# The order of score tiles and value products in the third window of each head

## What is computed

```python
q = (x @ w_q)...   # 32 heads of 128
k = (x @ w_k)...   # 8 key heads, each shared by 4 query heads
v = (x @ w_v)...
lk = ((x @ w_lq) @ w_lk)...   # 32 latent key heads
lv = (x @ w_lv)...            # 32 latent value heads
q, k, lk = rope(q), rope(k), rope(lk)
attn = causal_attn(q, k, v)      # softmax(q k^T * scale) v
lat = causal_attn(q, lk, lv)
return attn @ w_o + lat @ w_lo
```

## Time and profile before

| what | value |
|---|---|
| time, median of 3 runs | 2036.35 us (2035.51 to 2037.13) |
| profiled execution: time | 2036.75 us |
| profiled execution: span of the trace | 2035.0 us |
| PE / PEld busy | 99% / 86% of the span |
| DVE / ACT / POOL busy | 72% / 59% / 44% |
| mean granted TensorE clock | 0.998 |
| HBM traffic | 40 GB/s over the span |

### The profile page before, as it was taken

One profiled execution on the slowest core, in us unless ns is written; L12 is line 12 of the kernel. 1 busy time (PEld: TensorE's weight loads), 2 busy tenths in 40 slices (PEclk: granted clock), 3 DMA queues, 4 the chain that ended last, 5 costly groups with the idle time before them and its releaser, 6 DMA issues.

```text
span 2035.0 us, 33416 instructions
## 1 busy us (share of the span) xinstructions
PE 2018.2 (99%) x11716; PEld 1753.1 (86%) x11716; DVE 1457.1 (72%) x2884; ACT 1203.7 (59%) x2505; POOL 889.9 (44%) x684
## 2 busy tenths in 40 slices
PE   8999999999999999999999999999999999999989
PEld 7888888888888888888888888888888888888877
DVE  7677776776777767777677776777776776777777
ACT  4666556565565656666566565666566565565651
POOL 5444544444443454444534454444544444443422
PEclk9999999999999999999999999999999999999999
DMA  3111111111111111112111111111111111111031
GB/s 108 47 34 44 48 28 38 34 49 37 38 39 39 33 44 37 44 28 49 33 44 37 39 39 28 49 34 44 48 28 41 32 49 39 37 39 38 23 68 42
DMA packets 101797, 83.78 MB, mean 41 GB/s; under 512 B 28152, under 2 KB 73848, under 8 KB 101632
## 3 DMA queue, kind: packets, MB, share of 16 engines
q1 hardware_dynamic: 101632, 81.65, 15.7%
HBM read 79.26 MB, written 2.36 MB: 40 GB/s over the span
## 4 chain that ended last, share of the span: by engine, by line
PE 97%; DVE 2%; ACT 1%; POOL 0%; issue 0%; DMA 0%; DVEq 0%; ACTq 0%
PE bankT L587 13%; PE scores L514 12%; PE scores L516 12%; PE scores L515 12%; PE bankX L514 9%; PE bankX L516 9%; PE bankX L515 9%; PE bankO L516 7%; PE bankO L515 7%; PE bankO L514 7%; PE scores L707 0%; PE scores L553 0%; DVE rot_half L1124 0%; DVE xnT_lo L1097 0%; ACT probs L876 0%
## 5 line engine op out<-in xcount | busy, mean ns | idle before, releaser
L815 ACT ACTIVATE PT_hi<-bankT 128x512 fp32r<-128x512 f32 (+2 forms) x640 | 337.5, 533 | 310.7 <-PE bankO L516 275.5
L1113 DVE TENSOR_TENSOR PT_lo<-bankT,PT_hi 128x512 fp32r<-128x512 f32 (+2 forms) x640 | 388.1, 607 | 175.7 <-ACT PT_hi L815 173.1
L876 ACT ACTIVATE probs<-probs,nmax 128x128 f32<-128x128 f32 (+7 forms) x512 | 393.9, 771 | 129.8 <-DVE nmax L1107 129.7
L1107 DVE CUSTOM_DVE_ANT_0 probs<-scores,mask 128x128 f32<-128x128 f32 (+7 forms) x512 | 379.2, 750 | 69.3 <-PE scores L516 68.0
L587 PE MATMUL bankT<-ident,probs 128*128 128x128 f32 x2304 | 382.7, 275 | 6.8 <-ACT probs L876 5.0
L587 PEld LDWEIGHTS bankT<-ident,probs 128*128 128x128 f32 x2304 | 279.6, 140 | 67.9 <-DVE PT_lo L1113 11.7
L1369 POOL TENSOR_TENSOR rot<-rot,cos 128x512 f32<-128x512 f32 x144 | 186.9, 1298 | 256.6 <-DVE rot_half L1124 256.6
L1363 POOL TENSOR_TENSOR OT_lo<-o_raw,OT_hi 128x512 fp32r<-128x512 f32 x63 | 98.3, 1560 | 319.9 <-ACT OT_hi L815 319.9
L815 ACT ACTIVATE OT_hi<-o_raw 128x512 fp32r<-128x512 f32 x128 | 146.7, 1146 | 139.7 <-DVE o_raw L1182 139.7
L1371 POOL TENSOR_TENSOR rot<-rot,rot_half 128x512 f32<-128x512 f32 x144 | 199.9, 1388 | 11.3
L1123 DVE TENSOR_TENSOR rot_half<-rot,sin 64x512 f32<-64x512 f32 x144 | 99.5, 691 | 135.3 <-ACT rot L815 132.3
(11 more groups left out here) (304 smaller groups left out, 5334.0 us busy)
## 6 DMA issues: line engine op xcount, KB each, us to landing
inv_b<-inverses SPq DMA_DIRECT2D x128, 256.0 KB, 3.9
stage<-in_L_attn_w_q SPq DMA_DIRECT2D x32, 256.0 KB, 4.8
stage<-in_L_attn_w_lv SPq DMA_DIRECT2D x32, 256.0 KB, 2.9
stage<-in_L_attn_w_o SPq DMA_DIRECT2D x32, 256.0 KB, 3.5
stage<-in_L_attn_w_lo SPq DMA_DIRECT2D x32, 256.0 KB, 2.6
acc<-in_L_attn_hidden_states SPq DMA_DIRECT2D x8, 256.0 KB, 4.9
stage<-in_L_attn_w_k SPq DMA_DIRECT2D x8, 256.0 KB, 5.0
stage<-in_L_attn_w_v SPq DMA_DIRECT2D x8, 256.0 KB, 5.0
```

What stands on the lines that cost most here:

```text
L815: return act.activation(place, src, ACT.Copy)
L876: act.activation(prob_tile(c, t), prob_tile(c, t), ACT.Exp, bias=nmax[:, c, t:t + 1], scale=-1.0, accum_out=rsum[:, c, t:t + 1]).then_inc( ...
L1107: dve.tensor_tensor_reduce(place, src, tile_view(mask[:, S - width:S], c), -SCALE, -MASKED, ALU.add, ALU.min, nmax[:, c, t:t + 1]).then_in ...
L1113: dve.tensor_tensor(pt_place(1, hh, w, j), bankT[j % 2][:, block_columns(c, j):CH], f32(pt_place(0, hh, w, j)), ALU.subtract).then_inc(pt_ ...
```

## The change

The third row of the table changes: in window 2 the four score tiles are made in slots 0, 1, 1 and 2; before they were made in slots 0, 0, 1 and 1. This is the row that window 0 already has. The row is read by PE, DVE and ACT alike. No instruction is added or removed, and the orders of POOL and SP are the same.

```diff
-TILE_SLOTS = [[0, 1, 1, 2], [1, 2, 4, 6], [0, 0, 1, 1], [4, 4, 5, 6]]
+TILE_SLOTS = [[0, 1, 1, 2], [1, 2, 4, 6], [0, 1, 1, 2], [4, 4, 5, 6]]
```

## The result

| kernel | median, us | runs | ratio to before |
|---|---|---|---|
| before | 2037.05 (2035.51 to 2037.95) | 6 | |
| changed | 2056.06 (2054.7 to 2057.25) | 6 | 1.0095 (95% interval 1.0082 to 1.0108) |

The change makes the kernel 19.0 us slower. 2039.2 was forecast, at most 2043.0. The span of the profiled execution grew from 2035.0 to 2054.2 us.

What follows compares the result with a forecast made beforehand. PE, busy 99% of the span, was taken to bound the kernel, so only its waits count: 31 × (0.18 − 0.11) = 2.2 us plus 0.7 in the last head, 2.9 more, 2039.2 against 2036.35; range 2035.0 to 2043.0.

Steps and rivals of the forecast that it cites:

- Tile 2's wait of 0.11 us: Window 2, load of tile 2 waiting for row_max of tile 0: the change removes it, gaining 0.11 us a window.
- the 0.19 that the prediction named as a sign: Window 2 of the changed kernel: T(2)'s two transposes should stand 0.19 us from the value product, against 0.13 before.
- T(3), PV(1), tile 3 and the next T(0): Later steps of window 2 and start of window 3: no new wait, 0.3 us to spare, next T(0) about 0.2.
- the sum of 2.9: Whole kernel: 31 windows × (0.18 − 0.11) = 2.2 us, and 0.7 in the last head, 2.9 us more.
- Added: a wait of T(2): Window 2, T(2) waiting for PT_lo of block 0: load 0.12 us late, uncovered transposes 0.06 more, cost 0.18 a window.
- at most 0.25: Upper bound on T(2)'s cost a window, if the value product behind it also finds its load uncovered by more.
- T(2)'s 0.18 us: Window 2: the cost a window taken for T(2)'s new wait, between bounds of 0.12 and 0.25.
- The last head: No Q piece there: tile 3 ends later by 0.64 + 0.07 = 0.71 us, going in full to the program's end.
- tile 2's wait went: Rival for window 2: tile 2 keeps its old 0.11 us wait beside the new 0.18, 2042.6 us; chance 10%.
- T(2)'s came: Rival for window 2: T(2)'s new wait is hidden whole because PT_lo comes sooner, 2033.6 us; chance 5%.
- the next T(0) did not wait: Rival: the next T(0) waits for tile 3's late exponential, 0.1 us beyond the slack costing 3.1: 2042.3 us; chance 7%.
- an uncovered load does cost: Rival for T(2) in window 2: an uncovered load costs nothing, new wait only 0.12 us, 2037.4 us; chance 8%.

Runs made afterwards that it cites:

- e6: Kernel before, with DVE's row_max of tile 0 of window 2 ahead of the low part of block 1: 2032.88 us, ratio 0.9981.
- e5: Changed kernel, with DVE doing scale_out before the low part of block 0 at the end of window 1: 2048.25 us, ratio 1.0059.
- e1: Kernel before, with only tile 3 of window 2 moved behind T(3) and PV(1), tile 1 staying in slot 0: 2037.43 us, ratio 1.0005.
- e11: e3, with DVE doing row_max of tile 1 before the low part of block 2, as in the kernel before: 2039.64 us, ratio 1.0014.
- e4: Changed kernel, with scale_out of window 1 on 128 of bankO's 512 columns in all heads but the first (output wrong): 2043.02 us, ratio 1.0031.
- e2: Kernel before, with only tile 1 of window 2 moved behind T(2) and PV(0), tile 3 staying ahead of T(3): 2105.54 us, ratio 1.0340.
- e3: Changed kernel, with PE alone issuing tile 1 of window 2 between T(2) and PV(0), ACT and DVE keeping the changed order: 2045.03 us, ratio 1.0042.

## Why the prediction was wrong

*What held.* PE bounds the kernel, and only its waits count. Tile 2's wait of 0.11 us went (e6: 0.10 to 0.12). T(2) waits 0.13 us for PT_lo, forecast 0.12, and its two transposes take 0.19 us where nothing else holds what follows them (1059.59 to 1059.79 in e5; 0.19 to 0.20 in its heads). In the changed kernel itself PV(0) stands 0.69 us behind them, not the 0.19 that the prediction named as a sign. T(3), PV(1), tile 3 and the next T(0) brought nothing: e1 and the unchanged windows 0, 1 and 3. With the forgotten wait taken out, the sum of 2.9 stands against 2.7 measured (e11).

*The step that failed* is "Added: a wait of T(2)". It named PV(0) as queued behind T(2) and asked only for PT_lo, the wait at L594. PV(0) of every window has a second one, two lines below in the same function: `pe.wait_ge(o_scaled, ...)`, since bankO is one bank and `scale_out` must have read the former window's sum out of it. The prediction named `scale_out` as work on DVE ahead of `row_max`, and never as something that PE waits for. Its row was in the trace, and by it bankO came free 0.38 us ahead of PV(0). The list of waits could not show it, as a wait that is over before its time leaves no entry. The bound "at most 0.25" was therefore none: it held for one of the two waits in front of PV(0). With 1.07 − 0.38 − 0.11 = 0.58 in place of 0.07 the same sum would have been 31 × 0.58 + 1.2 = 19.2 us.

*The two waits are no sum.* T(2)'s 0.18 us costs nothing beside PV(0)'s: PE stands still until o_raw whether it has waited for PT_lo or not. e4 and e5 show the trade.

*The last head.* Forecast 0.7, measured 1.19 (the fourth transpose of T(0) starts 9.76 us after tile 0, before 8.57). The terms were the right ones, T(3) and PV(1) and the net of the waits; the net was 0.55 and not 0.07.

*The rivals.* All four varied the size of waits that were already named, and none came true: tile 2's wait went, T(2)'s came, the next T(0) did not wait outside the last head, and an uncovered load does cost (e6). (The forecast's own range has slips of 0.2: its terms give 2038.0 and 2041.1 us, not 2037.8 and 2040.9. Nothing hangs on it.) The case that came true, another semaphore in front of a step that moves up, was not among them.

*The window that hid it.* Window 0 already has this row of the table, and no wait on o_raw shows in it. Its rows in the kernel before:

```profile
1024.10 0.68 DVE L1182 TENSOR_TENSOR o_raw<-bankO,inv_b 128x512 f32<-128x512 f32 x1
...
1024.94 0.48 PE L514 MATMUL bankO<-PT_hi,V_lo 128*128 128x512 f32 x1
```

1024.10 + 0.83 = 1024.93: PV(0) starts 0.01 us after bankO comes free (by the starts of 31 heads, 0.02), so the same wait has next to no slack there. The LK piece between tile 0 and T(2), three matmuls from 1024.11 to 1024.81, is its cover. Window 2 has no piece in slot 0.

## What to carry to other kernels

When a step moves forward, list every wait in front of it and of what follows it from the code, and look up when each was released in the old trace: the slack of each is its start less the release, and the cover that the change takes away is to be set against the smallest. A list of waits shows only those that end last, never the next. Two waits in front of one step cost the later one, not the sum; and an in-order engine that waits for a step which the change delays passes that on to everything behind it (e2, e3), so one table read by three engines is three changes.

## What was not expected of the hardware

A wait of 0.50 us of PV(0) shows as 0.25 in its matmul row (the row of the two transposes ahead, 0.44 us long, covers the rest) and as 0.46 with the word "issue" on its load, where the loads of T(2) and of tile 2 name the instruction that they waited for; a search for the releaser among the loads alone would not have found it. And a vector instruction on 512 columns held PE back until 0.74 to 0.75 us (PT_lo to the load of T(2)) and 0.83 us (o_raw to the first matmul of PV(0)) after its start, with 0.68 to 0.69 us of its own length.
